# A graph network's edge stages over 49 blocks of edges instead of 50

## What is computed

```
x = layernorm(x + layer(x, edge features, src, dst))
layer 0, 1, 3:  message of an edge = products of x[one end] with weights from a small network of the edge's features
                out = segment_sum(message, other end)           # 50,000 rows, added up by node
layer 2:        a = score of the edge; amax = segment_max(a, dst)
                w = exp(a - amax[dst]) / segment_sum(exp(a - amax[dst]), dst)
                out = segment_sum(value * w, dst), then a feed-forward block on every node
```

## Time and profile before

| | |
|---|---|
| median of 3 timed runs | 6494.27 us (6494.11 to 6495.6) |
| the profiled execution's own time | 6489.29 us |
| its span, first to last instruction | 6487.5 us |
| mean granted TensorE clock | 0.913 of full speed |
| instructions | 124927 |
| TensorE (PE) busy | 5139.3 us, 79% |
| VectorE (DVE) busy | 4269.7 us, 66% |
| ScalarE (ACT) busy | 2869.0 us, 44% |
| GpSimd (POOL) busy | 4415.7 us, 68% |
| moved by DMA | 850.72 MB, 131 GB/s over the span |

### The profile page before, as it was taken

The page is one execution under the profiler, slowest core; times in us unless marked ns, Lnnn a source line. Parts: engine busy times, 40 slices in busy tenths (PEclk is TensorE's granted clock), DMA queues, the critical chain, the costliest instruction groups (busy, mean ns, idle before and its releaser), DMA issues. The chain is left out here.

```text
span 6487.5 us, 124927 instructions
## 1 busy us (share of the span) xinstructions
PE 5139.3 (79%) x28257; PEld 3947.1 (61%) x28280; DVE 4269.7 (66%) x14852; ACT 2869.0 (44%) x6302; POOL 4415.7 (68%) x4689
## 2 busy tenths in 40 slices
PE   8899966669997997999655344438999989998676
PEld 6566656646666995677322134337888867776666
DVE  3566658854544886888677521217888878776788
ACT  5333347744443664444200000006777764443566
POOL 8688856658886897766377688875666657887222
PEclk9899989989998998999888766669999999999999
DMA  8566667746665763555311244443333324554665
GB/s 318 126 123 125 121 153 221 220 106 131 130 126 148 232 229 120 166 158 157 115 34 32 76 85 77 74 56 99 110 106 111 105 91 88 88 85 68 223 223 188
DMA packets 592231, 850.72 MB, mean 131 GB/s; under 512 B 220782, under 2 KB 340382, under 8 KB 587566
## 3 DMA queue, kind: packets, MB, share of 16 engines
q1 hardware_dynamic: 409646, 693.65, 33.6%
q0 software_dynamic: 182400, 154.98, 17.3%
HBM read 469.53 MB, written 377.54 MB: 131 GB/s over the span
## 5 line engine op out<-in xcount | busy, mean ns | idle before, releaser
L1140 POOL DMA_INDIRECT xg<-x,gidx x600 | 620.4, 1034 | 250.2 <-issue 184.9
L328 POOL DMA_INDIRECT agg<-summed,cidx x400 | 643.4, 1608 | 194.4 <-issue 113.6
L2017 PE MATMUL pc_a<-msg_a,same_a 128*128 128x168 f32 x1000 | 263.0, 450 | 411.9 <-ACT summed_a L2004 357.8
L2017 PEld LDWEIGHTS pc_a<-msg_a,same_a 128*128 128x128 f32 x1000 | 249.7, 305 | 425.8 <-issue 298.0
L401 DVE TENSOR_TENSOR pr<-pf,ws 128x512 f32<-128x512 f32 x200 | 138.3, 691 | 523.2 <-PE pf L488 399.7
L1151 POOL DMA_INDIRECT agg<-summed,cidx x200 | 322.7, 1613 | 79.7 <-issue 58.5
L1963 POOL DMA_INDIRECT agg<-summed_a,cidx_a x200 | 318.7, 1593 | 70.7 <-issue 59.7
L1314 ACT ACTIVATE ob<-po 128x416 f32<-128x416 f32 (+1 forms) x400 | 201.6, 504 | 359.8 <-PE po L1391 185.7
L1883 PE MATMUL pm_m<-arow_m,ones_m 128*128 128x512 bf16 x400 | 150.9, 466 | 236.7 <-DVE top_m L1830 234.6
L517 PEld LDWEIGHTS pc<-ob,same 128*128 128x128 f32 x2000 | 278.6, 190 | 79.5 <-issue 78.3
L2199 POOL TENSOR_TENSOR rs_n<-ve_n,wsb 128x4 f32<-128x4 f32 x98 | 98.7, 1007 | 333.8 <-DVE nm_n L2187 331.8
(11 more groups left out here) (354 smaller groups left out, 17754.1 us busy)
## 6 DMA issues: line engine op xcount, KB each, us to landing
ar_n<-agg SPq DMA_DIRECT2D x194, 322.0 KB
agg<-zero SPq DMA_DIRECT2D x50, 768.0 KB
ar_n<-agg SPq DMA_DIRECT2D x97, 384.0 KB
agg<-zero SPq DMA_DIRECT2D x50, 672.0 KB
ar_n<-agg SPq DMA_DIRECT2D x97, 336.0 KB
agg<-zero_h SPq DMA_DIRECT2D x25, 1288.0 KB, 5.4
agg<-zero SPq DMA_DIRECT2D x50, 644.0 KB
x<-xn_n SPq DMA_DIRECT2D x97, 324.0 KB, 2.7
```

What stands on the lines that cost most here:

```text
L328: pool.indirect_dma_start(agg, bass.IndirectOffsetOnAxis(ap=cidx[r][:, t:t + 1], axis=0), summed[u][:, t, :], None, compute_op=ALU.add).th ...
L1140: pool.indirect_dma_start(xg[s][r][:, t, 0:XR], None, x, bass.IndirectOffsetOnAxis(ap=gidx[s][r][:, t:t + 1], axis=0)).then_inc(gathered[r ...
L2017: last = pe.matmul(pc[:, t, 0:W], same[u][:, s, t * P:(t + 1) * P], msg[u][:, s, :], start=(s == t), stop=(s == T - 1))
```

## The change

NB, the number of blocks that the edge stages run over, becomes 49. A new constant NBH = NB + 1 = 50 takes its place wherever the number 50 has to stay: the input arrays (NBP = 51), the share of a table that one zeroing covers, the pairs of the hidden stage, the tables it writes, and the edge lengths. Since 49 zeroings no longer cover the next table, SP issues a fiftieth behind its pipeline in layers 0, 1 and 2. In layer 2 the wait for the stores counts 25 in the first buffer and 24 in the second.

```diff
-NB = 50
-NBP = NB + 1
+NB = 49
+NBH = NB + 1
+NBP = NBH + 1
...
-ZS = NA // P // NB
+ZS = NA // P // NBH
...
-            sp.wait_ge(cleared, 16 * NB)
+            sp.dma_start(later.rearrange("(p r) c -> p (r c)", p=P)[:, NB * ZS * AW[l + 1]:NBH * ZS * AW[l + 1]], zero[:]).then_inc(cleared, 16)
+            sp.wait_ge(cleared, 16 * NBH)
...
-                sp.wait_ge(cleared, 16 * NB)
+                sp.dma_start(later.rearrange("(p r) c -> p (r c)", p=P)[:, NB * ZS * AW[3]:NBH * ZS * AW[3]], zero[:]).then_inc(cleared, 16)
+                sp.wait_ge(cleared, 16 * NBH)
                 for u in range(2):
-                    sp.wait_ge(kept[u], 16 * (NB // 2))
+                    sp.wait_ge(kept[u], 16 * ((NB + 1 - u) // 2))
...
-    NP = NB // 2
+    NP = NBH // 2
...
-        ylen = ctx.enter_context(nc.sbuf_tensor("ylen", [P, 2, NB // 2 * YP], F32))
+        ylen = ctx.enter_context(nc.sbuf_tensor("ylen", [P, 2, NBH // 2 * YP], F32))
...
-        dram["hid"] = table("hid", NB * 64, B)
-        dram["hid3"] = table("hid3", NB * 64, B)
+        dram["hid"] = table("hid", NBH * 64, B)
+        dram["hid3"] = table("hid3", NBH * 64, B)
```

## The result

The kernel before takes 6494.27 us (median of 5 runs, 6493.31 to 6499.02), the changed one 6461.81 us (median of 5, 6456.21 to 6468.58). The ratio is 0.9948, interval 0.9934 to 0.9963: faster by 0.5%, 32 us. The prediction was 6421 us with a range from 6409 to 6437, so the time lies outside it. The forecast saved 73 us; 41 of them are missing.

The account below looks back on a forecast made before the run. No single engine bounds the whole; by stage, GpSimd's indirect DMAs or, in layer 2, TensorE. Saving 75.3 - 1.8 - 0.4 = 73.1 us from 6494.3 gives 6421 us, 1.13% faster, range 6409 to 6437.

Parts of the forecast that it names:

- What goes: Six edge and attention stages: one unrolled full-load step, number 49, disappears from each, saving 75.3 us in all.
- What would show it: New trace: six stages 10 to 13.6 us shorter; wrong if drains grow, clock falls, or node stages change over 2 us.
- rival C: All stages: less than a step saved, at contention's price, 67.0 us, giving 6427; counted within the forecast's 91%.
- Zeroing, layer 2: End of layer 2: another 768 KB behind the last zeroing adds 1.8 us on the path, bounds 0 and 3.6.
- hidden fixed part: Layer 2 zeroing: 1.8 us if the DMA's fixed part of about 2.0 us hides behind the DMA in front, else 3.8.
- Zeroing, layer 1: Layer 1 drain: a fourth back-to-back zeroing delays the scatter-add behind it by 0.4 us, bounds 0 and 1.8.
- Zeroing, layer 0: End of layer 0: GpSimd's last four adds, 7.4 us, cover the added zeroing; cost 0, or 1.8 without cover.
- Rival A: Stage ends: only a drain step is saved, 53.7 us net, giving 6440.6 us; chance 6%.
- The other chain: Layer 0 drain: one add waited 4.43 us instead of 2.84, taken as a sign that another chain is near.
- Rival B: TensorE in node stages: half clock eats the gain, each us costing 0.54; 6583 us at 300 us low; chance 2%.
- a granted clock below 1.00: Dense node stages: named as the trace sign that would prove the forecast wrong in favour of rival B.
- Rival D: Edge-block loops: the fiftieth, padding block is needed elsewhere, so the time stays the same; chance 1%.

Follow-up runs that it names:

- after: The changed kernel (49 blocks in place of 50) against the kernel before: 6461.81 us, ratio 0.9948.
- 60 fillers: The changed kernel plus 60 unread semaphore increments behind VectorE's pipeline of the layer 1 edge stage: 6422.14 us, ratio 0.9889 to the kernel before.
- again: The changed kernel run once more, unchanged, against the kernel before: 6466.86 us, ratio 0.9955.
- 60 again: The changed kernel with the same 60 semaphore increments, run once more: 6421.89 us, ratio 0.9885 to the kernel before.
- lengthened layer 2 loop: Changed kernel with 60 fillers, plus six a step in VectorE's layer 2 node stage: 6513.08 us; with 60 further fillers ahead of that stage: 6433.07 us.

## Why the prediction was wrong, step by step

- **What failed:** the part "What goes" priced the removal of the unrolled step 49 only by its time, the hardware loops standing where they stood. Nothing in the sum, in the rivals or in the range held a price for code that moves. In its place the runs show VectorE's loop of 283 instructions fetched again at nine branches: layer 1's node stage took 487.4 us with 56 packets on q14, against 446.3 with 12, and 60 idle instructions ahead of it took that back (448.2 and 447.0). The claim in "What would show it" that node stages stay within 2 us was the test that failed. Layer 2's node stage is 2.7 to 3.6 us longer in the four kernels below as well, in after with the same 12 packets; that is not explained. The rest of the miss is small, since the same kernel with 60 fillers gives 6422.14 and 6421.89 us.
- **The size of the step:** the mechanism held in all six stages. Over the four kernels after, again, 60 fillers and 60 again (each against the one profile of before), the mean savings are 11.2 us in layer 0 (forecast 13.4), 11.3 in layer 1 (12.6), 9.2 in layer 2 (10.3), 9.5 in attention max (10.2), 13.9 in attention sum (13.0) and 14.3 in layer 3 (13.6), in all 69.4 (64.5 to 73.5) against 73.1. The lowest lies under the 67.0 of rival C. Layer 0 is the term most off: I took the 13.39 of one pair of adds, which lies above the mean of 13.0 by the earlier trace rows.
- **Zeroing, layer 2:** +1.8 forecast; SP's wait grew by 2.0 (1.8 to 3.8), and the stage ends 9.9 us behind its last store instead of 8.0. Right. The transfer of 768 KB adds its own length once more, as it does behind another transfer. The Trainium skill (DMA: Bandwidth & Descriptors, "Anatomy of one DMA") gives its sum of a fixed part and bytes for DMAs that GpSimd issues, which the prediction doesn't say; these are SP's. Taken over to them, an estimate, its reading with a hidden fixed part agrees with the trace: 3.8 us for two, and not 5.6.
- **Zeroing, layer 1:** +0.4 forecast. In the profile of after the drain took 64.1 us, before 60.2; in the repeat 63.4, with 60 fillers 62.2. So 2 to 4 us against 0.4, a term that was mis-sized. It has two parts. The add behind the zeroings, which waited 3.09 us in the kernel before with three of them, waited 4.68, 4.98, 4.34 and 5.08 in after, again and the two with 60 fillers, and 3.17 when the fourth was moved to the stage's start: so the fourth zeroing costs 1.3 to 2.0 us, about my bound of 1.8. The rest is the first add of the drain (4.95, 4.18, 3.26 and 2.83 against 2.71). In the first three a 16 KB packet of the queue q8, another instruction queue, began 2.9 to 3.6 us ahead of that add (in after at 1960.9, for 0.96 us), in the fourth 1.3 us ahead. That these packets delay the landing is read from the traces and wasn't tried.
- **Zeroing, layer 0:** 0 forecast. Nothing in the drain speaks against it, but the stage saved 9.4 to 14.4 us in four kernels, so 1 or 2 us can't be seen.
- **Rival A** (only a drain step goes): out. The six stages saved 64.5 to 73.5 us in the four kernels, its own price being 53.7. In the profile of after alone layers 0 and 1 come close to its terms (9.4 and 9.3 us); there the first add of the drain waited 4.02 and 4.95 us, and in 60 again the same stages gave 14.4 and 12.7. The other chain that A spoke of is there now and then, not always.
- **Rival B** (the clock): the granted clock did fall, 0.98 to 0.95 in the node stage of layer 1, and the time was lost there. It is a consequence: TensorE waits behind VectorE nine times. The lengthened layer 2 loop shows the same, 0.95 when it is fetched again and 0.99 when not, with the same instructions, and there the lower clock makes up about half of the loss. The price also has a slip: 0.54 is what one us of full-speed work costs more at the low level; of each us spent there 0.35 is lost (1 - 273/421). I named "a granted clock below 1.00" as the sign of B, which would have led me to the wrong cause; the sign that tells them apart is who idles first, and on what.
- **Rival D** (the step doesn't go): out. The scatter-adds count 392 and 196 after, where the earlier trace rows has 400 for two layers.
- **The start:** the first stage was 4.9 us shorter in the profile of after. In the other kernels timed beside a before of 6495 or 6496 us it was 0.2 to 3.1 us shorter, so most of it is scatter.

The Trainium skill (Runtime: NRT & Kernel Launch, "Instruction fetch mechanics") has the rule that speaks against this change, and I did not weigh it: a taken branch to code that is not held stalls the engine. The traces agree with the stall (4.66 us behind the branch). They disagree with its block of 16 KiB for VectorE: packets of 8 KB and a period of 128 instructions decide. The page has two blocks held, 32 KiB in all. At its 64 bytes an instruction the loop of 283 is an estimate of 18 KB, and by the page it would be lost only where it reaches into a third block of 256. The runs show it lost wherever it touches a fourth block of 128.

The best kernel measured with certainty is the changed one with 60 fillers, 6422 us: it beats the kernel before by 1.1% and the changed one by 0.6%.

**Open:** where b comes from; why five packets and not four are fetched a turn (in one turn of after they start at 2181.2, 2183.7, 2186.8, 2201.4 and 2215.6, the last 1 us ahead of the next branch, so it may be the block behind the loop); why twelve fillers cost 12 us more than three; the 7.5 us in layer 2's node stage of the kernel before with fillers; the late landing in layer 1's drain.

## What to carry to other kernels

Before pricing an edit that adds or removes unrolled code, list the hardware loops behind it on each engine with their lengths, and ask which of them are near the size that the engine can hold; for VectorE here a loop of 283 to 286 instructions was held at some starts and not at others, and a loop of 262 was never lost. In a trace, the mark is idle time of several us at the first instruction of every turn, put down to "issue" or to another engine, with more packets on the engine's instruction queue; a few dozen idle instructions ahead of the loop, where the engine waits anyway, test it and cure it. When a change gains less than it should, cut both spans by stage first: the loss here lay in a stage that the change never touched.

## What the runs showed of the hardware

- Instructions come over queue q14 in packets of 8 KB. A loop of VectorE that is not held costs five packets a turn. In layer 1's node stage VectorE then idles 3.8 to 5.2 us at each branch back (6.6 to 7.4 with twelve fillers), and 0.7 to 0.8 when the loop is held. In the lengthened loop of layer 2 it idles 3.1 to 3.4 us against 0.6, and the stage loses 4.0 us a branch.
- The position counts modulo 128 instructions: 122 and 126 fast, 62, 65, 66 and 74 slow for 283 instructions, and 128 fillers change nothing.
- A comparison with an accumulated output takes two places in VectorE's program.
- Filler instructions cost nothing where the engine waits anyway: 60 of them ran in 5.5 us and 196 in 18.8 us of a wait of 33 us.
- A zeroing of 768 KB costs 1.8 to 2.0 us each when several stand in a row at the end of a stage; ahead of the loop it put layer 2's first store off by 2.6 to 3.1 us. A fourth zeroing of 672 KB among scatter-adds cost the add behind it 1.3 to 2.0 us.
